# A vision tower with attention and routed experts on one core: loads, token halves, denominators and the order of the tail

## What is computed

```python
h = patches @ W_proj.T + b_proj + pos_emb            # (16, 36, 256)
h = concatenate([cls_tok, h], axis=1)                # 37 tokens an image, 592 in all

def attention(x):                                    # 4 heads of 64
    q, k, v = x @ Wq.T, x @ Wk.T, x @ Wv.T
    attn = softmax(causal(q @ k.T)) @ v              # within an image
    sq = elu(q) + 1
    A_mem = (sq @ mem) / (sq @ z + 1e-6)             # mem 64 x 64, z 64 x 1 of each head
    g = sigmoid(betas)
    return (g * A_mem + (1 - g) * attn) @ Wo.T + bo

def experts(x):                                      # 8 experts, top 2, 185 rows each
    xn = layernorm(x) * gamma + beta
    logits = clip(xn @ router_w.T)
    top_p, top_i = softmax(top_2(logits))
    slot = rank of the token among those that chose the same expert, in order of tokens
    y = w3[e] @ (silu(gate) * up),  gate, up = halves of w12[e] @ xn     # F = 1024
    return sum of top_p * y over the two experts, for tokens with slot < 185

h = h + attention(layernorm(h))
h = h + experts(layernorm(h))
```

## Time and profile before

| | |
|---|---|
| runs shown | 247.74, 249.91, 249.59 us; median 249.59 us |
| the profiled execution | 245.9 us, of which 244.1 us is the span from its first to its last instruction |
| mean granted clock of TensorE | 0.923 |
| busy time of PE | 215.2 us, 88% of the span |
| busy time of DVE, ACT, POOL | 88.9, 76.0, 47.2 us |
| chain of work that ended last | PE 71%, DVE 8%, DMA 7%, POOL 4%, issue 4%, ACT 3% |
| 512 expert matmuls of L575 | 93.1 us |
| 256 expert matmuls of L587 | 50.2 us |

### The profile page before, as it was taken

How to read it: one execution, slowest core, us unless ns; L and a number is a source line. 1 busy time by engine, 2 the same in 40 slices (tenths; PEclk the granted TensorE clock), 3 DMA queues, 4 the chain that set the end, 5 groups by cost and what they waited for, 6 DMA issues and landing times.

```text
span 244.1 us, 3582 instructions
## 1 busy us (share of the span) xinstructions
PE 215.2 (88%) x1317; PEld 189.4 (78%) x1317; DVE 88.9 (36%) x285; ACT 76.0 (31%) x224; POOL 47.2 (19%) x46
## 2 busy tenths in 40 slices
PE   1929999699879768599999999999999999999970
PEld 0729988367657344299999999999999999999960
DVE  7557947987882444012311111111111111111120
ACT  3342337446630012115322332322222322222220
POOL 2013400000062445000004013031040040220404
PEclk9976999979995665979999999999999999999997
DMA  6956995520021211469048076094390670410101
GB/s 240 281 197 133 326 344 233 219 102 10 27 67 56 62 51 49 112 174 341 5 179 339 3 303 226 11 422 117 133 390 5 262 273 0 172 12 0 23 10 17
DMA packets 10465, 36.15 MB, mean 148 GB/s; under 512 B 3370, under 2 KB 6776, under 8 KB 8144
## 3 DMA queue, kind: packets, MB, share of 16 engines
q1 hardware_dynamic: 7680, 32.95, 37.3%
q0 software_dynamic: 2336, 2.13, 4.5%
q10 hardware_dynamic: 432, 0.85, 1.0%
HBM read 31.42 MB, written 5.35 MB: 151 GB/s over the span
## 4 chain that ended last, share of the span: by engine, by line
PE 71%; DVE 8%; DMA 7%; POOL 4%; issue 4%; ACT 3%; POOLq 1%; SPq 0%; ACTq 0%
PE bank L575 34%; PE bank L587 16%; DMA w_sb<-in 4%; PE bank L559 3%; POOL token_rows L1099 3%; PE bank L496 2%; DMA x_flat<-in 2%; PE bank L346 2%; PE bank L485 1%; PE bank L347 1%; PE bank L348 1%; PE bank L600 1%; PE bank L440 1%; ACT x_flat L733 1%; DMA token_rows<-rowbuf,dest 1%
## 5 line engine op out<-in xcount | busy, mean ns | idle before, releaser
L575 PE MATMUL bank<-xb,w 128*128 128x185 f32 x512 | 93.1, 326 | 1.1 <-ACT xb L779 1.1
L575 PEld LDWEIGHTS bank<-xb,w 128*128 128x128 f32 x512 | 83.5, 193 | 1.6 <-issue 1.2
L1062 DVE TENSOR_TENSOR hid<-bank,sg 128x185 f32<-128x185 f32 x64 | 22.5, 351 | 115.9 <-ACT sg L791 115.9
L587 PE MATMUL bank<-hid,w 128*128 128x185 f32 x256 | 50.2, 319 | 0.0
L791 ACT ACTIVATE sg<-bank 128x185 f32<-128x185 f32 x64 | 20.9, 327 | 90.8 <-PE bank L575 90.8
L1116 POOL DMA_INDIRECT out<-yw,slot_token x16 | 23.8, 1490 | 119.9 <-ACT yw L811 110.7
L587 PEld LDWEIGHTS bank<-hid,w 128*128 128x128 f32 x256 | 42.1, 189 | 0.0
L346 PE MATMUL bank<-wp_hi,x_hi 128*111 128x256 f32 x36 | 11.9, 330 | 4.4 <-DVE x_lo L866 4.4
L1099 POOL DMA_INDIRECT token_rows<-rowbuf,dest x12 | 11.6, 967 | 19.6 <-DVE dest L1016 17.4
L346 PEld LDWEIGHTS bank<-wp_hi,x_hi 128*111 128x111 f32 x36 | 7.2, 201 | 5.2 <-issue 5.2
L347 PE MATMUL bank<-wp_lo,x_hi 128*111 128x256 f32 x36 | 11.0, 306 | 0.0
(11 more groups left out here) (146 smaller groups left out, 259.4 us busy)
## 6 DMA issues: line engine op xcount, KB each, us to landing
w<-in SPq DMA_DIRECT2D x8, 2048.0 KB, 10.7
w<-in SPq DMA_DIRECT2D x8, 1024.0 KB, 4.8
x_flat<-in SPq DMA_DIRECT2D x6, 333.0 KB, 8.4
token_rows<-rows_in SPq DMA_DIRECT2D x1, 1728.0 KB
rows_in<-token_rows SPq DMA_DIRECT2D x8, 144.0 KB
w_sb<-in SPq DMA_DIRECT2D x1, 1024.0 KB, 9.8
wp_sb<-in ACTq DMA_DIRECT2D x2, 384.0 KB, 5.0
out<-h SPq DMA_DIRECT2D x5, 111.0 KB
```

The source lines that it names most:

```text
L575: mm = pe.matmul(o, w[:, part, k, :], xb[b][:, k, :], start=(k == 0), stop=(k == KD - 1))
L587: mm = pe.matmul(bank[YT_BANK[k]][:, 0:NS], w3[e % 2][:, fc, k * P:(k + 1) * P], hid[:, step % 4, :], start=(fc == 0), stop=(fc == FC - 1))
L1062: dve.tensor_tensor(hid[:, step % 4, :], bank[GU_BANK[step % len(GU_BANK)]][:, NS:2 * NS], sg[:, step % 2, :], ALU.mult).then_inc(hid_done, 1)
```

## The change

The change has five parts; lines with a plus are those of the changed kernel.

1. **Loads.** x groups from 2 on are each issued behind the landing of the group two before; `w_sb` is loaded in three pieces: value weights (a quarter) behind x 2 and x 3, query and key weights (a half) behind x 4, output weights (a quarter) behind x 5. ACT and DVE wait for the piece that they split; the first `project` waits for the third piece.
2. **Halves.** The first half of the tokens is 334 columns and the second 258, so that the first holds groups 0 to 2 and one more column.
3. **Denominators.** `memory_den` now has the tokens as rows: `sqT` is the stationary side, `z_sb` gives 4 columns, two matmuls a group. DVE adds 1e-6, inverts 111 x 12 values and splits them into high and low columns; PE turns these 8 columns a group (`turn_den`), ACT copies the result (`turn_copy`), and `memory` spreads it with one matmul in place of two.
4. **Front.** The keys of the first half stand ahead of the last value on PE, and `memory_den(0)` ahead of the projections of the second half; it waits for the last value's copy. ACT copies the first queries and keys within its loop; DVE makes the first half's features around the last split of `hnT`, with the addition of `bo` ahead of them. `memory(3)` and its copy move by one stage.
5. **Tail.** DVE's order from step 8 on changes, POOL sends group t - 3 behind the root of group t, and `keep_busy` has 7 passes.

```diff
-HALF = T // 2
+HALF = GROUPS // 2 * G_ROWS + 1
...
+        MEM_HALF = (slice(0, HALF - 2), slice(HALF - 2, T))
+        DEN_HALF = (slice(0, GROUPS // 2 * G_ROWS), slice(GROUPS // 2 * G_ROWS, T))
+        HALF_GROUPS = (range(0, GROUPS // 2), range(GROUPS // 2, GROUPS))
...
-            sp.wait_ge(in_x[0], 16)
-            sp.dma_start(x_sb[:, 2, :, :], xT[2]).then_inc(in_x[2], 16)
-            sp.dma_start(w_sb[:, :, :, :], wqkvoT).then_inc(in_w, 16)
-            sp.wait_ge(in_x[1], 16)
-            for g in range(3, GROUPS):
+            for g in range(2, GROUPS):
+                sp.wait_ge(in_x[g - 2], 16)
                 sp.dma_start(x_sb[:, g, :, :], xT[g]).then_inc(in_x[g], 16)
+                if g == 3:
+                    sp.dma_start(w_sb[:, 2, :, :], wqkvoT[:, 2, :, :]).then_inc(in_w[0], 16)
+                if g == 4:
+                    sp.dma_start(w_sb[:, 0:2, :, :], wqkvoT[:, 0:2, :, :]).then_inc(in_w[1], 16)
+            sp.dma_start(w_sb[:, 3, :, :], wqkvoT[:, 3, :, :]).then_inc(in_w[2], 16)
...
+                if t == GROUPS + 2:
+
+                    pe.wait_ge(w_hi_done, 3)
+                    pe.wait_ge(w_lo_done, 3)
+                    for n in range(2):
+                        project_in(1, n)
                 if t >= 3:
                     value(t - 3)
...
-                for m in range(2):
-                    mm = pe.matmul(bank[PT_BANK][0:HEADS, 0:HALF], z_sb[:, m, :], sqT[:, m, half(hf)], start=(m == 0), stop=(m == 1))
+                for g in HALF_GROUPS[hf]:
+                    for m in range(2):
+                        mm = pe.matmul(bank[PT_BANK][0:ROWS[g], g * HEADS:(g + 1) * HEADS], sqT[:, m, cols(g)], z_sb[:, m, :],
+                                       start=(m == 0), stop=(m == 1))
...
+            def turn_den(hf):
+
+                pe.wait_ge(den_done, hf + 1)
+                for n, g in enumerate(HALF_GROUPS[hf]):
+                    R = ROWS[g]
+                    tr = pe.transpose(bank[(PV_BANK, PT_BANK)[hf]][0:2 * HEADS, n * G_ROWS:n * G_ROWS + R],
+                                      den_split[0:R, g, :, :].bitcast(F32).rearrange("p s h -> p (s h)"), ident[0:R, 0:R])
+                tr.then_inc(denT_in_psum, 1)
...
-                pe.matmul(bank[PV_BANK][:, 0:HALF], head_rows_r[:, m, :], denT_hi[:, half(hf)], start=True, stop=False)
-                pe.matmul(bank[PV_BANK][:, 0:HALF], head_rows_r[:, m, :], denT_lo[:, half(hf)], start=False, stop=True).then_inc(gate_in_psum, 1)
+                pe.matmul(bank[PV_BANK][:, 0:W], head_rows_r[:, m, :], denT[:, tokens], start=True, stop=True).then_inc(gate_in_psum, 1)
...
-            keep_busy(5)
+            keep_busy(7)
...
+            invert_den(1)
             row_max(1)
-            invert_den(1)
-            for t in range(GROUPS + 7):
-                for lag, stage in ((5, residual), (4, add_memory), (1, row_max), (6, rank), (5, norm2), (6, send), (2, normalise)):
+            for t in range(GROUPS + 6):
+                if t < GROUPS + 2:
+                    order = ((5, residual), (4, add_memory), (1, row_max), (6, rank), (5, norm2), (6, send), (2, normalise))
+                elif t == GROUPS + 2:
+                    order = ((5, residual), (4, add_memory), (4, residual), (3, add_memory), (5, norm2), (6, rank), (6, send))
+                else:
+                    order = ((5, norm2), (4, residual), (6, rank), (6, send))
+                for lag, stage in order:
...
-            for t in range(GROUPS + 1):
+            for t in range(GROUPS + 3):
...
-                if t >= 1:
-                    send(t - 1)
+                if t >= 3:
+                    send(t - 3)
```

172 lines of the change are left out of this document (103 added, 69 removed).

## The result

| | median | of | range |
|---|---|---|---|
| before | 248.67 us | 4 executions | 246.88 to 249.91 |
| changed | 235.72 us | 4 executions | 233.95 to 240.02 |
| changed, a second series | 235.53 us (before: 248.39 beside it) | 6 executions | 231.59 to 239.64 |

The ratio is 0.946 with a 95% interval of 0.933 to 0.959, and 0.939 (0.930 to 0.947) in the second series: 13 us saved where 8.3 were forecast; 235.72 lies just inside the range of 235 to 246. Executions of the changed kernel differ by up to 8 us, so two profiles of it are read here, one of 240.02 us (span 238.2), called the low one, and one of 235.5 us (span 232.7), called the high one: TensorE's clock falls early in the tail of the low one and not in that of the high one.

What follows compares the result with a forecast made beforehand. It took PE's experts as untouched and the gap before the third group, attention's front and the tail as movable. Savings of 1.1 + 1.7 + 4.7 + 0.8 = 8.3 us from 249.59 gave 241.3 us, range 235 to 246.

Steps and rivals of the forecast that it cites:

- The loads: Start of the kernel, gap before the third group's embedding: value weights as an earlier quarter load, 1.1 us saved.
- the first rival: Loads: x lands early when fewer bytes share the queue, third embedding under 14 us, whole 236.2 us; chance 0.07.
- The front: Start of attention, from about 41 us: waits, spread matmuls and low clock removed, small matmuls added; 1.7 us saved.
- Two additions: Start of attention: 12 small memory_den matmuls forecast to add 1.1 us, six transposes of the denominators 1.0 us.
- The 0.8 for the spreads and the 1.3 for the clock: Start of attention: 0.8 us saved by four fewer low-half matmuls, 1.3 us by less time at the lower clock.
- The slower rival: Start of attention: many 4-column matmuls bring the lower clock and it stays, +8 us there, whole 254.7 us; chance 0.04.
- The tail: Ranking and sending of tokens: new DVE and POOL order starts the last sends earlier; 4.7 us saved, taken as the middle.
- The upper end: Ranking and sending of tokens at 2.4 GHz: POOL's sends in a row are the bound; 7.6 us saved.
- The lower end: Ranking and sending of tokens at 1.2 GHz: PE's chain is the bound; 1.8 us saved.
- signs of being wrong: PE waiting over 1 us at memory_den(0), ACT for group 4 or its weights, or tail's lower-level runs staying as long.
- The hand-over: Wait for the first tokens before the experts: two more keep_busy passes hold the clock; 0.8 us saved.
- The base: Whole kernel before the change: median 249.59 us taken as starting time, 3.7 higher than the profiled execution of 245.9.

## Why the prediction was right, step by step

**The loads** (1.1 us forecast, 1.8 by the rows). The few engines that carry pos and bias were the right bound: their two pieces moved what was said to hold x group 2, and the first rival, that x comes early once fewer bytes share the queue (embedding under 14), did not happen without them. But the sentence that the weights did not delay x group 2, and that moving them won't bring it earlier, was wrong: it landed 6.8 us behind its issue for 7.7. So the value weights, forecast at 13.98, were split at 13.26, and PE started 2.31 us behind that, for the 2.33 of the forecast.

**The front** (1.7 forecast, 3.3 measured). Two additions were sized too high. The 12 matmuls of `memory_den` were put at 3.4 us by a row with 8 columns; they take 1.19 and 1.10, as much as the four wide ones (2.3), so the 1.1 us for them are nothing. The transposes were put at 1.0 and cost 0.29 and 0.41. The wait for the last value's copy was 0.47 for 0.5. With these the sum is 0.7 + 1.45 + 0.8 + 1.3 - 0.7 - 0.5 = 3.05. The 0.8 for the spreads and the 1.3 for the clock are not measured one by one.

**The slower rival** was judged rightly, and by the right reason, but its weight was missed. It was said to fail because projections stand between the two `memory_den`. Taking those away from between the first one and the scores gave 249.1 us in the median, with one execution of six at 237.18: the forecast for it was 254.7, its 8 us in the front were 7.1. In the prediction this place was half a sentence; of all that was undone it is worth the most.

**The tail** (4.7 forecast, as the middle of 1.8 and 7.6). The upper end was right to 0.2 us, and so was its bound: 7.4 us, eight sends in one row, 1.24 apart. Neither profile is in the middle: they have 7.4 and 0.3. Seven of the ten executions of the changed kernel timed lie at 231.6 to 237.4 us, three at 239.2 to 240.0. The lower end was sized too low for the order, which is worth 2.7 us where both orders run at the lower level, and missed that the level can fall earlier than before (63.4 for 73.3 us), which takes 2.4 back (43.27 - 40.83) and leaves 0.3. By one of the prediction's own signs of being wrong, runs at the lower level that stay as long as they were, the low profile speaks against it: the clock is 0.50 to 0.53 there from 63.4 to 95 us, for 20.5 us at that level before.

**The hand-over** (0.8 forecast; 0.5 won in the low profile, 1.2 lost in the high one): the step that failed. It took the clock's fall behind the wait for the tokens to depend on two more passes. Five and seven took the same time in the medians, and the first 24 matmuls were slow in either case (5.69 behind five before, 6.92 behind seven) or quick (4.01 behind five, 4.01 behind seven). The loss it allowed for came in the low profile, where the passes at the lower level ended behind the tokens' arrival.

**The base.** The profile taken of before (245.9 us) was among its fastest executions, so it was right to add to it. The 3.7 us were 0.9 too many: the median was 249.59 with the three runs shown and 248.67 with the fourth. So the forecast of 241.3 was 5.6 us too high by 0.9 in the base and by 4.7 in the savings (13.0 for 8.3).

**The range.** That 235.72 still lies in it, by 0.7 us, is in part luck. Its lower end was put there for the first rival, which did not come; the front and the tail's upper end brought the time there. Four of the ten executions lie under 235.

## What to carry to other kernels

Where the rows show the granted clock falling behind small matmuls and a wait, try wide work that is due anyway between them: here one call moved by a few lines cost the front 7.1 us in the profile and the median more than any other thing undone. When a step can end in one of two levels, forecast one of them with its chance rather than the mean, and read more than one profile. And look at what is queued behind a transfer that runs on few engines: with 96 + 15 rows for 111 the next load landed 2.8 us sooner behind its issue, and the last send came 1.8 us earlier.

## What the runs showed of the hardware

The same kernel, with the same busy times and waits for 20 us, went on at 1.2 GHz in one execution and at 2.4 in another (63.4 us on, 0.51 and 1.00), so a profile shows one draw. The same load of 333 KB landed 7.6, 6.8 and 4.0 us behind its issue, as 1 MB behind it and two transfers of 111 rows ahead of it were cut up. With the tokens as stationary side and 4 columns, six float32 matmuls cost 1.19 us, for 1.7 worked out from the nearest row of before. And undoing either of two orders alone cost 4.9 and 5.7 us by the medians, undoing both only 3.4.
